# Nine products that nobody reads, ahead of the fifth query tile's first near scores in an attention head loop

## The reference, cut to what matters

```python
def _attn(q, k, v, mask=None):
    s = jnp.einsum('bhqd,bhkd->bhqk', q, k) / np.float32(np.sqrt(HD))
    if mask is not None:
        s = jnp.where(mask, s, jnp.float32(-1000000000.0))
    return jnp.einsum('bhqk,bhkd->bhqd', jax.nn.softmax(s, -1), v)
...
o1 = _attn(q, k1, v1, causal[None, None])
...
o2 = _attn(q, ks, vs)
...
winmask = causal & (ii[:, None] - ii[None, :] < WINDOW)
o3 = _attn(q, kw, vw, winmask[None, None])
g = gate[:, :, None, None, None]
o = g[:, 0] * o1 + g[:, 1] * o2 + g[:, 2] * o3
```

## Time and profile before

| | |
|---|---|
| median of 3 runs | 2758.36 us (2757.94 to 2763.6) |
| the profiled execution's own time | 2755.48 us |
| its span in the trace | 2751.5 us |
| TensorE busy | 2476.1 us (90%) |
| VectorE / ScalarE / GpSimd busy | 1885.7 / 1462.4 / 1309.9 us |
| mean granted clock of TensorE | 0.944 |
| first and last `near.4.0` of the 16 passes | 755.75 and 2447.50 us from the span's start |

### The profile page before, as it was taken

One profiled execution on the slowest core, in us unless ns is written; L12 is line 12 of the kernel. 1 busy time (PEld: TensorE's weight loads), 2 busy tenths in 40 slices (PEclk: granted clock), 3 DMA queues, 4 the chain that ended last, 5 costly groups with the idle time before them and its releaser, 6 DMA issues. The chain is left out here.

```text
span 2751.5 us, 52837 instructions
## 1 busy us (share of the span) xinstructions
PE 2476.1 (90%) x17187; PEld 1731.3 (63%) x17187; DVE 1885.7 (69%) x3715; ACT 1462.4 (53%) x2524; POOL 1309.9 (48%) x884
## 2 busy tenths in 40 slices
PE   5599996765899999999999999999999999999777
PEld 3466664554566666666666666666666666666766
DVE  2767764667486776877767768677686776877526
ACT  1124553332366657666576665666666657666223
POOL 0213681000245637557375573664746647457235
PEclk8699998877999999999999999999999999999788
DMA  3003310011431121120211202122112121120242
GB/s 113 1 12 87 68 26 9 1 46 58 112 87 43 33 51 35 43 55 15 51 35 43 55 15 51 35 47 51 29 38 44 38 51 35 43 55 15 74 139 69
DMA packets 85079, 131.61 MB, mean 48 GB/s; under 512 B 16224, under 2 KB 60769, under 8 KB 84625
## 3 DMA queue, kind: packets, MB, share of 16 engines
q1 hardware_dynamic: 81328, 123.16, 17.7%
q0 software_dynamic: 3024, 7.43, 0.8%
q10 hardware_dynamic: 656, 0.09, 0.0%
HBM read 63.49 MB, written 20.79 MB: 31 GB/s over the span
## 5 line engine op out<-in xcount | busy, mean ns | idle before, releaser
L2467 ACT ACTIVATE a_PT<-PS 128x512 f32<-128x512 f32 (+1 forms) x1111 | 613.7, 586 | 343.0 <-PE PS L2330 235.5
L2188 POOL TENSOR_TENSOR a_KT<-a_PT 128x512 f32<-128x512 f32 (+2 forms) x179 | 418.5, 2353 | 466.0 <-ACT a_PT L2467 464.0
L2188 POOL TENSOR_TENSOR a_KT<-a_KT,a_PT 128x2048 f32<-128x2048 f32 (+3 forms) x128 | 391.8, 3061 | 8.8
L2536 DVE TENSOR_REDUCE a_NM<-PS 128x2 fp32r<-128x512 f32 x460 | 297.1, 687 | 120.2 <-PE PS L2280 116.5
L2329 PE MATMUL PS<-a_QH,a_KSW 128*128 128x256 f32 (+2 forms) x848 | 305.2, 379 | 7.1 <-ACT a_PT L2467 7.1
L2329 PE MATMUL PS<-a_QH,a_K 128*128 128x512 f32 (+3 forms) x768 | 306.9, 406 | 0.0
L2550 DVE TENSOR_REDUCE a_MX<-PS 128x1 f32<-128x512 f32 (+3 forms) x432 | 267.3, 665 | 39.2 <-PE PS L2291 21.2
L2330 PE MATMUL PS<-a_QL,a_K1B 76*128 76x512 f32 (+3 forms) x768 | 262.1, 348 | 0.0
L2291 PE MATMUL PS<-a_K,a_QH 128*128 128x512 f32 (+3 forms) x768 | 253.2, 397 | 0.0
L2277 PE MATMUL PS<-a_KSW,a_QH 128*128 128x512 f32 x460 | 196.2, 476 | 29.4 <-DVE a_QL L2520 29.4
L2523 DVE TENSOR_TENSOR a_KSW<-PS,a_KSW 64x512 fp32r<-64x512 f32 x170 | 117.2, 690 | 126.6 <-ACT a_KSW L2426 123.4
(11 more groups left out here) (437 smaller groups left out, 5573.1 us busy)
## 6 DMA issues: line engine op xcount, KB each, us to landing
a_KWB<-a_KSW SPq DMA_DIRECT2D x68, 256.0 KB, 3.3
a_K1B<-a_K SPq DMA_DIRECT2D x32, 512.0 KB, 5.3
a_XC<-latents SPq DMA_DIRECT2D x17, 512.0 KB, 3.9
a_CKS<-latents SPq DMA_DIRECT2D x17, 512.0 KB, 4.6
a_CF<-latents SPq DMA_DIRECT2D x17, 448.0 KB, 4.1
slots<-in_empty_slots SPq DMA_DIRECT2D x1, 5160.0 KB, 18.7
f_XB<-slots SPq DMA_DIRECT2D x8, 645.0 KB, 8.9
c_EX<-in_experts SPq DMA_DIRECT2D x1, 4608.0 KB, 17.3
```

The costliest lines, as they stand in the source:

```text
L2188: nc.gpsimd.tensor_tensor(total, one_in, other_in, ALU.add).then_inc(s["added"], 1)
L2467: nc.scalar.activation(PT[:, to:to + width], turning(key)[:, 0:width], ACT.Exp).then_inc(s["taken"], 1)
L2536: ins = nc.vector.tensor_reduce(out, bank.rearrange("p (a n) -> p a n", a=2), AX.X, ALU.max, negate=True)
```

## The change

`near_scores` now makes TensorE wait in two pieces instead of one: first for its bank, then for the low parts of the queries. Between the two, for query tile 4 and head 0 alone, nine of the products of `keep_clock` are issued into the bank that the near scores will use. `near.4.0` is a step of the loop only, so there are nine more products in each of 16 passes, 144 in all.

```diff
                     made = {0: ("s", "w0", "q0"), 2: ("w1", "q1"), 4: ("q2",), 6: ("q3",)}[i] if h == 0 and i % 2 == 0 else ()
-                    after(pe, q, at, bank_free(key, q), *(("reduced", ("split", "tr", g)) for g in made))
                     bank, k0, w = ring(key), max(0, i - 1) * 128, 256 if i else 128
+                    after(pe, q, at, bank_free(key, q))
+                    if i == 4 and h == 0:
+                        keep_clock(9, bank)
+                    after(pe, q, at, *(("reduced", ("split", "tr", g)) for g in made))
...
-                def keep_clock(count):
+                def keep_clock(count, bank=P[7]):
...
                     for _ in range(count):
-                        nc.tensor.matmul(P[7][:, 0:384], identb[:, :], masks.rearrange("p a n -> p (a n)"), start=True, stop=True)
+                        nc.tensor.matmul(bank[:, 0:384], identb[:, :], masks.rearrange("p a n -> p (a n)"), start=True, stop=True)
```

## The result

The changed kernel takes 2771.55 us (median of 20 runs, 2763.06 to 2779.54), the kernel before 2761.15 us (20 runs, 2750.46 to 2772.59). The ratio is 1.0037, with an interval of 1.0026 to 1.0049: 7 to 13.5 us more, where 2777 us and +0.7% had been forecast. Single executions of the kernel before lie up to 22 us apart, those of the changed one up to 16 us, which turns out to be part of the answer. The trace of the changed kernel is of an execution of 2772.2 us, with a span of 2767.5 us.

A forecast was written before the change was run, and what follows sets the result against it. TensorE was taken to bound the head loop, busy 109.64 of 112.60 us a pass. Delay of 13.5 us plus 5.5 us of clock falls, 19.0 us on the 2758.4 us median, gave 2777 us, 0.7% slower; range 2768 to 2786.

The forecast's parts named there:

- The products stand behind the wait, and the idle 1.64 us stays whole: At near.4.0, one event frees the bank and the low parts, so the products start at 1096.07, after the 1.64 us wait.
- A product holds TensorE for 0.162 us, nine for 1.46: Price of the products ahead of near.4.0, from 62 in a row in the trace: 0.162 us each, 1.46 us for nine.
- 0.67 us of it is taken up by score.4.3's wait: The wait for ScalarE's exponentials absorbs 0.67 us in thirteen passes, 0.37 in three; 13.5 us of delay remain over the loop.
- A delay here is not taken up later: After score.4.3, the near-maxima wait and next pass's split wait move along, absorbing hardly any of the remaining 0.79 us.
- Clock: +5.5 us: In the head loop, five clock falls at 1.6 us each, less 2.5 us already in the kernel before: +5.5 us.
- My reason for more falls: Passes made 0.8 us longer with the wait unchanged break the repetition of spared passes, so more than two falls come.
- Rival B: Products behind the near.4.0 wait make TensorE denser and all clock falls go: +11.0 us, 2769 us; chance 0.10.
- Rival D: Bank freed early, so the nine run inside the near.4.0 wait: 0 to -2.5 us, 2756 to 2758 us; chance 0.03.
- Rivals C and E: C: ten or more loop clock falls, 2785 to 2795 us, chance 0.08. E: later wait absorbs the rest, 0 to +4 us, 0.04.

The follow-up runs named there:

- e1_bank7_nine: The change's nine products issued into bank 7 ahead of the wait for the split, instead of behind it; 2754.19 us, ratio 0.9967 to the kernel before.
- e7_both: The change, plus nine more products in bank 7 ahead of the wait; 2764.06 us, ratio 1.0011 to the kernel before.
- e4_sixth_tile: The change with its nine products moved from ahead of near.4.0 to ahead of near.5.1, behind its wait; 2805.55 us, ratio 1.0149 to the kernel before.
- o8_turn_early_own_bank: Like o5_turn_early, but early turning ahead of a.q3, turning and split of tiles 6 and 7 directly ahead of near.4.0, near.4.1 one step earlier; 2805.45 us, ratio 1.0170.
- o9_turn_early_other_bank: Like o8_turn_early_own_bank in placing the early turning ahead of a.q3, but turning of tiles 6 and 7 first in the pass; 2753.70 us, ratio 0.9969.
- o5_turn_early: Kernel before, no added products; query tiles 4 and 5 turned ahead of the previous pass's final values, split ahead of its normalisation; 2746.87 us, ratio 0.9958.
- o6_turn_early_wk_late: As o5_turn_early, with the rounding of the key weights (step wk) also moved behind near.4.0; 2748.17 us, ratio 0.9959.

## Why the prediction was right in kind and too high

- *The products stand behind the wait, and the idle 1.64 us stays whole.* Right: 26.1 us of waiting before and after, and `e1_bank7_nine` shows the same nine for nothing in front of it.
- *A product holds TensorE for 0.162 us, nine for 1.46.* The single price held (eighteen against nine: 114.62 - 113.17 = 1.45 us more a pass). The nine delayed the next score by 1.37 us and not 1.46: about 0.09 us are gained where the near product follows a running row instead of an idle engine.
- *0.67 us of it is taken up by score.4.3's wait.* The late start of `score.4.3` is 0.68 us where 1.37 - 0.67 = 0.70 were due. But by `score.5.0` another 0.1 us had gone. I had read the distance of 0.57 us between the two as the length of a pair; in the trace after, the pair takes 0.47. The difference lies in the first product of the pair, as the rows below this list show: before, it came out of the wait and held the engine for 0.34 us (1097.69 to 1098.03); after, it follows a running one and holds it for 0.23 (1097.20 to 1097.43). A product that starts out of a wait costs about 0.1 us more, and neither the near product nor this one does so any longer; the sum had left that out. Delay per pass: 0.57 us, not 0.79; over 16 passes, three of them with 0.3 us more, 16 x 0.62 = 9.9 us instead of 13.5.
- *A delay here is not taken up later.* Right, to 0.01 us: `near.4.1` is 0.56 us late, and the next pass 0.57.
- *Clock: +5.5 us.* This term of the sum failed, more in its base than in the changed kernel. Five falls were forecast for the change; its trace has three, and the comparison with `e7_both` gives 7 us, which is four or five at 1.6 us. What I subtracted, 2.5 us for the kernel before, was read from one fortunate execution; the second trace has 9.5 us, and filling the wait is worth 4 to 9 us to that kernel. The two sides about cancel: the average time at 1.2 GHz is 317 us after and 316 to 323 before, and the average time less half of that is 2612.9 us after and 2601.1 to 2602.4 before, 10.5 to 11.8 us more. The sum is then 9.9 + 0, against the measured 10. Both terms were too high, so the forecast of 19 us is nearly twice the measured difference; that the time still lies within the stated range is due to its width.
- *My reason for more falls*, that a longer pass breaks the repetition of the spared ones, is not borne out for the change: none of its first eight passes had a fall, and the falls came in the ninth, thirteenth and sixteenth. It may be what happened in `e4_sixth_tile` and `o8_turn_early_own_bank`, but no run separates that.
- *Rival B* (the products keep the clock) is false where they stand, three falls at the products themselves, and true once they stand in the wait. The Trainium skill's page "TensorE: Matmul & The Clock Gate", section "What's actually happening", has activity release the throttled state; the traces agree as far as the 48 passes go. Rival D would have needed another bank: `e1_bank7_nine` is that kernel.
- *Rivals C and E* fell: the trace has three falls and not ten, and a pass at full clock takes 113.17 us and not 112.6.

The products of `score.4.3` and `score.5.0`, before (fourth pass) and after:

```profile
1097.69 0.50 PE L2329 MATMUL PS<-a_QH,a_KSW 128*128 128x512 f32 x1 [0.54 <-ACT a_PT L2467]
1098.03 0.40 PE L2330 MATMUL PS<-a_QL,a_KSW 76*128 76x512 f32 x1
1098.26 0.42 PE L2329 MATMUL PS<-a_QH,a_KSW 128*128 128x512 f32 x1
```

```profile
1097.20 0.39 PE L2332 MATMUL PS<-a_QH,a_KSW 128*128 128x512 f32 x1
1097.43 0.40 PE L2333 MATMUL PS<-a_QL,a_KSW 76*128 76x512 f32 x1
1097.67 0.40 PE L2332 MATMUL PS<-a_QH,a_KSW 128*128 128x512 f32 x1
```

**Open.** Why four products behind the wait measure best of the fillers (0.9957, with a 112.6 us pass as before and two falls in its trace). Its low clock over the whole run was the smallest, 291 us by the median of mean clocks, against 322 us for the kernel before on that chip, 305 for nine in bank 7. The four leave the second wait shorter; that this is the reason was not tried. Some of the gain may lie outside the loop: over the first 740 us, where the products do not stand, the granted clock is 0.86 in its trace and 0.85 in both of the kernel before. Open too is what decides, beside the waits, which passes have a fall.

## What to carry to other kernels

Before filling a wait, look up which event ends it, and whether the bank or buffer that the filler needs is released by that same event; if so, the filler stands in series and only a resource freed earlier lets it into the gap. Filler in front of the wait was free and kept the clock up (0.33% here with nine products, 0.15% and not clear of noise with fourteen); the same filler behind it cost all that the next wait on another engine didn't take up. Before a term is worked out from how often the clock fell in one trace, take a second trace of the same kernel.

## What the runs showed of the hardware

The clock fell close behind waits of 1.6 to 1.9 us, and in `o9_turn_early_other_bank` behind one of 1.1 and one of 0.6 us, far from an idle engine: TensorE was busy for 97% of the pass. How often this happens hangs on more than the wait: the two traces of the kernel before end with thirteen and ten spared passes of 112.6 us on average, four products behind the wait had two falls after four such passes, `o5_turn_early` and `o6_turn_early_wk_late` have a wait of 1.4 us and no fall in 32 passes, and two different kernels whose clock falls in every pass but the first run at nearly the same length, 116.06 us in `o8_turn_early_own_bank` and (115.05 + 117.08) / 2 = 116.07 us on average in `e4_sixth_tile`. Nine products that cost 1.45 us in a pass at full clock thus went with passes that were 3.5 us longer. A product of 512 columns that starts out of a wait held TensorE for 0.34 us, one that follows a running product of its kind for 0.23. Executions of one kernel on one chip differ by up to 24 us, and the loops of its two traces by 7 us through the clock.
